# Second layer of a two-layer attention network: VectorE's and ScalarE's share of the FFN norm moved behind the next tile's first maxima and first probabilities

## What is computed

```python
x = x + _L1_xattn_ref(_layernorm(x), ctx_4096, wq, wk, wv, wo, ln_w)   # RMS norm, 32 heads of width 16, softmax over 64 keys
x = x + _L1_ffn_ref(_layernorm(x), W_gate, b_gate, W_e, b_e)
...
    logits = x @ W_gate + b_gate
    _, top_idx = jax.lax.top_k(logits, 2)
    y_all = jax.nn.relu(jnp.einsum('bsd,edh->bseh', x, W_e) + b_e)      # all 8 experts
    y = jnp.take_along_axis(y_all, top_idx[..., None], axis=2)
    return y.mean(axis=2)
```

## Time and profile before

| | |
|---|---|
| time, median of 3 runs | 1885.27 us (1885.04 to 1886.22) |
| the profiled execution's own time | 1885.55 us |
| its span, first to last instruction | 1883.8 us |
| busy: PE, DVE, ACT, POOL | 95%, 66%, 48%, 26% |
| mean granted TensorE clock | 0.986 of full |
| first attention output of layer 1 added (L1894) | 1303.2 us after the span's start |

### The profile page before, as it was taken

The page is one execution under the profiler, slowest core; times in us unless marked ns, Lnnn a source line. Parts: engine busy times, 40 slices in busy tenths (PEclk is TensorE's granted clock), DMA queues, the critical chain, the costliest instruction groups (busy, mean ns, idle before and its releaser), DMA issues. The chain is left out here.

```text
span 1883.8 us, 36264 instructions
## 1 busy us (share of the span) xinstructions
PE 1781.2 (95%) x14128; PEld 983.3 (52%) x14128; DVE 1236.2 (66%) x2288; ACT 900.6 (48%) x1433; POOL 495.4 (26%) x370
## 2 busy tenths in 40 slices
PE   5989999999999999999999999977999999999997
PEld 2545555555555555555555444443555555555553
DVE  6785565646565646566566577758777877877863
ACT  5544444343434343434444333243666666666662
POOL 0161832505207034076000000000223322322324
PEclk9989999999999999999999999989999999999999
DMA  5011220301204012034100300004100000000000
GB/s 229 23 45 46 86 95 23 124 2 69 79 1 143 4 47 101 1 112 147 57 2 1 118 1 1 0 11 170 51 7 7 7 13 7 7 13 7 7 12 12
DMA packets 18376, 88.79 MB, mean 47 GB/s; under 512 B 2608, under 2 KB 2864, under 8 KB 10160
## 3 DMA queue, kind: packets, MB, share of 16 engines
q1 hardware_dynamic: 18224, 86.58, 12.7%
HBM read 65.60 MB, written 20.97 MB: 46 GB/s over the span
## 5 line engine op out<-in xcount | busy, mean ns | idle before, releaser
L642 PE MATMUL bank<-R 128*128 128x512 f16 (+1 forms) x7152 | 1304.7, 341 | 23.7 <-issue 7.1
L642 PEld LDWEIGHTS bank<-R 128*128 128x128 f16 x7152 | 584.4, 99 | 659.7 <-issue 40.9
L1490 DVE SCALAR_TENSOR_TENSOR R<-bank,biases,R 128x512 f16<-128x512 f32 x288 | 204.6, 746 | 249.8 <-ACT R L1095 209.0
L505 POOL TENSOR_TENSOR R<-R 128x512 f32<-128x512 f32 x112 | 156.2, 1395 | 430.2 <-ACT R L1286 428.9
L1095 ACT ACTIVATE R<-bank,biases 128x512 f16<-128x512 f32 x128 | 87.7, 686 | 235.2 <-PE bank L642 234.5
L396 POOL TENSOR_SCALAR R<-R 128x2048 f32<-128x2048 f32 (+1 forms) x20 | 33.8, 1692 | 435.9 <-PE bank L642 377.2
L1286 ACT ACTIVATE R<-R,msk 128x512 f32<-128x512 f32 x128 | 90.5, 717 | 49.3 <-DVE R L1824 49.3
L1502 DVE SCALAR_TENSOR_TENSOR R<-bank,R 64x512 f16<-64x512 f32 x64 | 44.0, 688 | 100.2 <-ACT R L1103 99.7
L1575 DVE SCALAR_TENSOR_TENSOR X<-bank,X 128x512 f32<-128x512 f32 x128 | 86.8, 683 | 34.7 <-PE bank L642 34.6
L642 PE MATMUL bank<-CT,R 128*128 128x512 f16 x384 | 91.6, 390 | 17.1 <-DVE CT L1464 11.8
L1824 DVE SCALAR_TENSOR_TENSOR R<-bank,R 128x512 f32<-128x512 f32 x128 | 87.1, 681 | 29.3 <-PE bank L642 28.3
(11 more groups left out here) (148 smaller groups left out, 2022.4 us busy)
## 6 DMA issues: line engine op xcount, KB each, us to landing
R<-in_wB SPq DMA_DIRECT2D x16, 1024.0 KB, 6.0
R<-in_wX SPq DMA_DIRECT2D x16, 1024.0 KB, 5.0
w_split<-AW SPq DMA_DIRECT2D x16, 1024.0 KB, 4.8
R<-w_split SPq DMA_DIRECT2D x12, 1024.0 KB, 7.2
R<-in_ctxT SPq DMA_DIRECT2D x4, 1024.0 KB, 10.0
X<-in_x SPq DMA_DIRECT2D x4, 1024.0 KB, 13.6
out<-X SPq DMA_DIRECT2D x16, 256.0 KB, 2.4
R<-in_wB SPq DMA_DIRECT2D x7, 512.0 KB, 5.6
```

The lines of the kernel that those rows point to most:

```text
L505: g.tensor_tensor(acc, acc, tmp[:, e % 2, :], ALU.add).then_inc(e_acc, 1)
L642: last = pe.matmul(dst, a(sa), b(sb_), start=(k == 0), stop=(k == m - 1))
L1490: v.scalar_tensor_tensor(out=dst, in0=src, scalar=bias, in1=hi, op0=ALU.add, op1=ALU.subtract).then_inc(done, 1)
```

## The change

VectorE. The call that normalizes tile n for the FFN (`norm_apply`) leaves the end of step n and becomes `ffn_norm(n - 1)` in step n+1, behind `less_max(n, 0)`. The low half (`ffn_lo`) and the eviction of expert 6 move from ahead of `row_sums(n, 0)` to behind `probs_lo(n, 0)`. ScalarE. The high half (`tile_hi`) leaves the end of step n and becomes `ffn_hi(n - 1)` behind `exponentials(n, 0)` of the next step. The store of the transposed tile (`norm_store`) moves ahead of expert 6. For the last tile both new calls stand directly behind step 15, so nothing moves there. TensorE, GpSimd and SyncE keep their programs.

```diff
@@ scalar @@
                 exponentials(n, 0)
                 if two:
+                    ffn_hi(n - 1)
                     expert(n - 2, 5)
+                norm_store(ffn_turn(n - 1), 1 - buf)
+                if two:
                     expert(n - 2, 6)
-                if one:
-                    norm_store(ffn_turn(n - 1), 1 - buf)
-                if two:
                     expert(n - 2, 7)
                 turned_p(n, 0)
                 exponentials(n, 1)
...
-                tile_hi(act, ffn_stat(n), 0, yn, ffn_turn(n - 1) + 1 if one else 33)
+
+            def ffn_hi(n):
+                tile_hi(act, ffn_stat(n), 0, yn, ffn_turn(n - 1) + 1)
...
             n = NT - 1
+            ffn_hi(n)
@@ vector @@
                 less_max(n, 0)
                 if two:
+                    ffn_norm(n - 1)
                     expert(n - 2, 5)
-                if two:
-                    ffn_lo(n - 1)
-                if two:
-                    expert(n - 2, 6)
                 row_sums(n, 0)
                 reciprocals(n, 0)
                 probs_lo(n, 0)
+                if two:
+                    ffn_lo(n - 1)
+                    expert(n - 2, 6)
                 if two:
                     expert(n - 2, 7)
                 less_max(n, 1)
...
+            def ffn_norm(n):
                 norm_apply(dve, ffn_stat(n), 0, x_tile(n), yn)
...
             attn_step(NT - 1)
+            ffn_norm(NT - 1)
             ffn_lo(NT - 1)
```

## The result

The changed kernel takes **1905.33 us**, median of 4 runs (1902.06 to 1907.81), beside 1885.74 for the kernel before in the same comparison (1885.04 to 1887.30). The ratio is 1.0102, with a 95% interval of 1.0084 to 1.0119: slower by some 19.6 us. The forecast was 1902, in a range of 1889 to 1906. The profiled execution took 1905.52 us, its span is 1903.7 and its mean granted clock 0.985.

The account below looks back on a forecast made before the run. VectorE's chain through the second low half was taken to bound the step. Twelve steps at 1.25 (15.0), 0.86 for step 10 and 0.4 for step 6 made 16.3 us on 1885.55: 1902, range 1889 to 1906.

Parts of the forecast that it names:

- What bounds the step: VectorE's chain to the end of the second low half, 17.26 after the first scores, sets the step of 35.50.
- TensorE's 10 us of waits are not the prize; VectorE's chain is: Layer 1: removing TensorE's 10.0 us of waits at L905 wins nothing while VectorE's chain to `weigh_v` decides.
- Step 10: Evidence from the kernel before: second low half ends 17.66 after first scores, step 35.89; 0.40 more on VectorE, 0.39 longer.
- The route: From the second low half through TensorE's transposes (L905) and ScalarE's copies (L1330) to `weigh_v`, 5.19 after it.
- The first stall: First low half of the probabilities (L1875): reaches the port before GpSimd, takes 1.21 instead of 2.10, saving 0.89.
- Who gets the port next: Behind the first low half, GpSimd's waiting addition goes ahead of L572, which ends at 9.48, taking about 1.7 instead of 0.68.
- one case in layer 0: GpSimd waited from 343.76; the second of two back-to-back VectorE subtractions took 1.64 instead of about 0.68.
- The rival in which VectorE keeps the port: At 7.80 VectorE keeps the port for L572, which ends at 8.40; the kernel is faster, 1878; chance 0.12.
- The second stall: VectorE's mask meets GpSimd's additions for expert 7 and to the tile; second low half 1.07 or 1.44 later.
- the regular step: Twelve of steps 2 to 15, each 1.25 longer, the middle of 1.07 and 1.44; 15.0 in all.
- Steps 6 and 10: The two odd steps: 0.4 more in step 6, 0.86 more in step 10.
- The signs that I had named: Timeline marks: second low half ending 18.3 to 18.7 after first scores, first scores 36.6 to 36.9 apart, among others.

Follow-up runs that it names:

- before_tile_add_late: The kernel before, with GpSimd's addition to the tile held back until the step's second low half is done; 1885.17 us, 0.9989 of the kernel before.
- reordered_tile_add_late: The changed kernel with VectorE's row sums and reciprocals moved behind the first low half and GpSimd's tile addition held back; 1880.09 us, 0.9965 of before.
- short_add_e5: The changed kernel with GpSimd's addition of expert 5 cut to 8 of 512 columns; 1892.94 us, 1.0042 of the kernel before.
- short_add_tile: The changed kernel with GpSimd's addition to the tile cut to 8 of 512 columns; 1891.74 us, 1.0035 of the kernel before.
- tile_add_late: The changed kernel with GpSimd's whole addition to the tile held back until the step's second low half is done; 1891.52 us, 1.0023 of before.
- scalar_order_back: The changed kernel with ScalarE's ReLU of expert 6 ahead of the store of the transposed tile again; 1898.32 us, 1.0068 of before.
- norm_moved_only: The changed kernel with VectorE's FFN low half, expert 6 and ScalarE's store put back, so only norm and high half move; 1898.28 us, 1.0071 of before.
- e6_before_lo: The changed kernel with VectorE's eviction of expert 6 put ahead of the FFN tile's low half (L572); 1903.40 us, 1.0095 of before.
- reordered: The changed kernel with VectorE's row sums moved behind the probabilities' low half, reciprocals behind the FFN tile's low half; 1895.52 us, 1.0049 of before.

## Why the prediction was right

**What bounds the step.** Held as a number; its route and one of its two witnesses did not. I read from steps 8 and 10 alone that the end of VectorE's second low half sets the step one to one. Over ten changed kernels it did, with 18.23 to 18.25 behind it while it moved between 16.96 and 19.33; the exception is before_tile_add_late. There TensorE's own path, with its wait at L905, was the longer one by 0.15. So "TensorE's 10 us of waits are not the prize; VectorE's chain is" was only half the truth: the two were level. Shortening VectorE's alone gave 0.02, and reordered_tile_add_late, where both are shorter, gives 0.30 a step. That is also why the sum of all waits said so little of the result.

Step 10 was a weak witness. I took from it that 0.40 more on VectorE made the step 0.39 longer. In before_tile_add_late the second low half of step 10 comes no later than in its other steps (17.11 after T0 = 1633.23), and the step is still 35.86, 0.38 longer than the others:

```profile
1637.15 2.76 PE L646 MATMUL bank<-R 128*128 128x512 f16 x12 [0.81 <-issue]
1649.12 1.22 DVE L1879 SCALAR_TENSOR_TENSOR R<-R 128x1024 f16<-128x1024 f32 x1
```

TensorE's late entry into its loop makes that step longer by itself. What carries the reading is the ten kernels, not step 10.

The route was read wrongly too. I sent the second low half through TensorE's transposes (L905) to ScalarE's copies (L1330). In step 8 of before the transposes start 0.38 behind the low half's end (1581.10), without a wait, and are done 1.77 before the copies start. The copies stand in ScalarE's order behind the ReLU of expert 1 of the tile before, and that one waits for VectorE:

```profile
1581.48 1.06 PE L905 MATMUL bank<-ident,R 128*128 128x128 f16 x16
1583.02 0.63 DVE L1824 SCALAR_TENSOR_TENSOR R<-bank,R 128x512 f32<-128x512 f32 x1
1583.68 0.72 ACT L1286 ACTIVATE R<-R,msk 128x512 f32<-128x512 f32 x1 [0.59 <-DVE R L1824]
1584.31 1.92 ACT L1330 ACTIVATE R<-bank 128x1024 f16<-128x1024 f16 x2
```

The same after:

```profile
1591.88 0.72 ACT L1286 ACTIVATE R<-R,msk 128x512 f32<-128x512 f32 x1 [0.59 <-DVE R L1827]
1592.51 1.92 ACT L1330 ACTIVATE R<-bank 128x1024 f16<-128x1024 f16 x2
```

So the path runs on through what VectorE has behind the low half: the eviction of expert 0, the scaling of the first attention output and its low half (with ScalarE's rounding between them), and the eviction of expert 1. All of it moves with the low half, which is why its end serves so well as a mark. It also says that the 0.62 for which TensorE waits at the second L905 after the change is not what lengthens the step: its transposes end at 1590.43, 2.08 before the copies start. That the copies would come earlier in another order of ScalarE's was not tried.

**The first stall.** L1875 takes 1.21, not 2.10: predicted, and measured 1.16. It was to end 7.80 after T0, and ended at 7.84.

**Who gets the port next.** The forecast stood on one case in layer 0: GpSimd, which waits, goes between two VectorE instructions that stand back to back. L572 was to take about 1.7 and end at 9.48; it took 1.75 and ended at 9.50. TensorE's L584 was forecast for 9.55 (9.63), the router product for 11.27 (11.37). short_add_e5 shows that it is this addition: with 8 columns L572 takes 0.68. The rival in which VectorE keeps the port, and the kernel is faster, fell here.

**The second stall.** The cast was to come at 14.02 and came at 14.03; the tile's addition from 14.8 to 16.05 ran from 14.89 to 16.17. Of the two cases, L1811 held (1.07) or L1807 ahead of it (1.44), it was the second. L572 took its 1.75 in all 14 steps. In 13 of them L1810 was held, for 1.29 or 1.30 in all; in step 2 it was L1809, the one ahead of it, for 1.32. short_add_tile and tile_add_late show that it is this addition, by its length and by its place.

The Trainium skill, page "SBUF — State Buffer", section "Who interferes with whom", had the second case: by it a `tensor_scalar` too can need the port pair that VectorE and GpSimd share under an exclusive lock. The trace agrees, with 1.30 instead of 0.22 for a tensor_scalar of eight columns.

**The term that was mis-sized.** I put the regular step at 1.25 more, the middle of 1.07 and 1.44. It was 1.57 in step 8 and 1.54 on average. 0.19 is the coin that fell to the long side. The other 0.13 comes from ScalarE: its ReLUs for experts 6 and 7 and GpSimd's additions behind them came 0.1 later than I had them (12.08 instead of 12.0 after T0, the pair 2.62 instead of 2.6), and the hold ends that much later. Steps 6 and 10 gave 0.22 and 1.16 where I had 0.4 and 0.86. With steps 2 to 15 at what was measured, 19.7 in all, the sum would have been 1905.3, beside 1905.5. The signs that I had named were passed as well: the second low half ends at 18.83 and not at 18.3 to 18.7, the first scores lie 37.07 apart and not 36.6 to 36.9. The median of 1905.33 is above the 1899.5 to 1904.5 of my own mechanism too, and inside the range by 0.7, out of the 2 us that stood there for collisions I couldn't place. That the range held is to that extent luck; that the kernel is slower, and by which two holds, is not. Of TensorE's waits, 0.90 before L584 (about 1.0 forecast) and 0.22 before the router product (0.3 to 0.4) came as named, and the 0.62 at the second L905 was not foreseen.

**ScalarE.** The forecast gave its new order no price of its own: the router product's 0.36 came from the later transposes, and the ReLUs behind the store only set when GpSimd's additions come. scalar_order_back shows what that is worth, 0.51 a step and 7 us in all, though the new order shortens TensorE's wait for the store from 9.5 to 3.1 us. It does so by where it puts GpSimd's additions.

What was not tried: another engine or another way to add the experts up, and an order in which ScalarE's store goes back while both collisions are avoided. That the low granted clock of single stretches comes from the idle time ahead of them is what the rows suggest, since a wait of 1.47 stood there and one of 1.66 ahead of the stretch in norm_moved_only, but e6_before_lo had the wait of 1.47 with twelve matmuls in 2.75 behind it. Its cause stays open.

## What to carry to other kernels

When two engines share a port, a collision shows as a long busy time of an instruction, in no view of waits. Compare the durations of like rows, and look for what the other engine did from its start to its end. Before moving work ahead of a stall, ask which engine is already waiting for the port and what stands directly behind the instruction that holds it: that one will pay, as L572 did here in all 14 steps. Put instructions there that read one operand from SBUF or from a bank, and hold back work of the other engine that nobody needs soon. And before spending on the longest wait, find out by one kernel whether a second path is level with it. A number that the step follows one to one need not be a link of the path: read in the rows what the next link really waits for.

## What the runs showed of the hardware

- An instruction's small size on VectorE did not spare it. Eight-column ones (a cast, a tensor_scalar, a tensor_tensor) were held 0.95 to 1.10 us by a GpSimd addition of 512 columns, and one of 512 columns (L572) 1.07. GpSimd's own addition of 8 columns took 1.01 beside a low half and 0.20 alone.
- A tenth of a microsecond chooses the victim. In after, step 8, L1809 started 0.13 ahead of the addition and took its usual 0.23, and L1810, which started 0.01 behind it, took 1.30. In step 2 L1809 started only 0.01 ahead of the addition (1362.86 beside 1362.87) and took 1.32.
- Instructions with one large operand in SBUF were not held: row sums took 1.21 beside a GpSimd addition of 1.27 (reordered, 1573.75 beside 1573.86), and expert 6's eviction, with its other operand in a bank, 0.68 while another addition ran (e6_before_lo, 1580.21 beside an addition that asked at 1579.33, waited out the low half until 1580.29 and ended at 1581.41).
